# Two reorderings at once in a fused attention and mixture-of-experts kernel: the attention's first units with the later norms, and the expert stage's places

## The reference

```python
mod = (silu(c) @ wmod).reshape(4, 6, 1, 256)            # sa, ca, ga, sb, cb, gb
ga, gb = clamped gates: sign * max(|g|, 0.25)
h = layernorm(x) * (1 + ca) + sa
x = x + ga * attention(h)       # 16 heads of 128, causal, softmax, then W_O
h = layernorm(x) * (1 + cb) + sb
x = x + gb * ffn(h)
# ffn: down 256->128, router with 8 experts (top 2 of a softmax), a shared
# expert, 8 experts of hidden width 128..512 with gelu before and after w1,
# their sum weighted by the gates, up 128->256, plus gelu(h) @ core
```

## Time and profile before

| | |
|---|---|
| median of 3 runs | 800.54 us (799.82 to 801.06) |
| time of the profiled execution | 800.14 us |
| its span | 798.2 us |
| PE busy in the span | 776.1 us (97%) |
| weight loads (PEld) | 690.7 us (87%) |
| DVE busy | 662.0 us (83%) |
| ACT busy | 624.9 us (78%) |
| POOL busy | 462.6 us (58%) |
| PE on the chain that ended last | 79% |

### The profile page before, as it was taken

The page is one execution under the profiler, slowest core; times in us unless marked ns, Lnnn a source line. Parts: engine busy times, 40 slices in busy tenths (PEclk is TensorE's granted clock), DMA queues, the critical chain, the costliest instruction groups (busy, mean ns, idle before and its releaser), DMA issues.

```text
span 798.2 us, 14365 instructions
## 1 busy us (share of the span) xinstructions
PE 776.1 (97%) x4700; PEld 690.7 (87%) x4700; DVE 662.0 (83%) x1649; ACT 624.9 (78%) x1449; POOL 462.6 (58%) x389
## 2 busy tenths in 40 slices
PE   8899999999999999999999999999999899989997
PEld 7689989999999999999999999999999677768786
DVE  4779998878888878888878888879898988786967
ACT  3787889877777888777888877887879868866974
POOL 2454456765557666555576655575445365677654
PEclk8999999999999999999999999999999999999999
DMA  7252233442223444223343332344222131112231
GB/s 250 83 171 69 67 93 96 113 105 67 67 67 71 101 111 120 70 67 70 84 106 93 93 93 69 85 110 133 69 67 67 48 119 55 53 41 68 75 98 53
DMA packets 47593, 70.53 MB, mean 88 GB/s; under 512 B 5536, under 2 KB 38464, under 8 KB 47392
## 3 DMA queue, kind: packets, MB, share of 16 engines
q1 hardware_dynamic: 47008, 68.81, 32.9%
q0 software_dynamic: 368, 0.81, 0.3%
q10 hardware_dynamic: 144, 0.00, 0.0%
HBM read 25.49 MB, written 2.17 MB: 35 GB/s over the span
## 4 chain that ended last, share of the span: by engine, by line
PE 79%; ACT 8%; DVE 7%; issue 3%; POOL 2%; DMA 1%; SPq 0%; DVEq 0%; POOLq 0%
PE M L759 12%; PE M L760 12%; PE M L758 12%; PE T L758 8%; PE T L760 8%; PE T L759 8%; PE S L758 5%; PE S L760 5%; PE S L759 5%; PE M L864 2%; ACT PB L696 1%; ACT PB L647 1%; PE S L849 1%; POOL stage L565 1%; DMA PB<-in_wmod 1%
## 5 line engine op out<-in xcount | busy, mean ns | idle before, releaser
L604 POOL TENSOR_TENSOR ptl<-ptl,pth 128x896 fp32r<-128x896 f32 x126 | 179.7, 1448 | 94.7 <-ACT pth L726 94.7
L696 ACT ACTIVATE PB<-PB,ri 128x256 f32<-128x256 f32 (+3 forms) x256 | 123.2, 553 | 30.4 <-DVE ri L1180 30.3
L647 ACT ACTIVATE PB<-S,nb 128x128 f32<-128x128 f32 (+3 forms) x256 | 135.2, 540 | 7.1 <-DVE nb L1171 6.9
L1160 DVE TENSOR_TENSOR qk<-M,qk 128x512 fp32r<-128x512 f32 x108 | 74.2, 687 | 58.8 <-ACT qk L711 58.7
L592 POOL TENSOR_TENSOR X<-X,fb 128x512 f32<-128x512 f32 x64 | 83.2, 1300 | 61.1 <-DVE fb L1207 61.0
L1171 DVE CUSTOM_DVE_ANT_0 S<-S,cc 128x128 f32<-128x128 f32 (+3 forms) x256 | 117.3, 520 | 1.3 <-PE S L760 1.3
L711 ACT CAST qk<-M 128x512 fp32r<-128x512 f32 x108 | 64.3, 595 | 67.0 <-PE M L760 67.0
L1187 DVE STREAM_TRANSPOSE gab<-PB 128x256 f32<-128x256 f32 (+2 forms) x192 | 109.5, 624 | 6.7 <-DMA ptl<-gab 2.2
L760 PE MATMUL M<-hh,W 128*128 128x512 f32 x222 | 87.5, 394 | 0.0
L759 PE MATMUL M<-hl,W 128*128 128x512 f32 x222 | 87.3, 393 | 0.0
L758 PE MATMUL M<-hh,W 128*128 128x512 f32 x222 | 86.8, 391 | 0.5 <-DVE hl L1146 0.5
(11 more groups left out here) (264 smaller groups left out, 2491.8 us busy)
## 6 DMA issues: line engine op xcount, KB each, us to landing
ptl<-gab SPq DMA_DIRECT2D x256, 160.0 KB, 3.1
stage<-in_wat SPq DMA_DIRECT2D x16, 512.0 KB, 5.1
gab<-scw SPq DMA_DIRECT2D x16, 256.0 KB, 3.2
tmp<-scw SPq DMA_DIRECT2D x16, 256.0 KB, 3.4
X<-in_x SPq DMA_DIRECT2D x3, 512.0 KB, 8.2
stage<-in_wfa SPq DMA_DIRECT2D x3, 512.0 KB, 4.8
out<-X SPq DMA_DIRECT2D x3, 512.0 KB, 2.6
X<-in_wmod SPq DMA_DIRECT2D x1, 1024.0 KB, 12.1
```

What stands on the lines that cost most here:

```text
L604: pool.tensor_tensor(pt_part(lo, c), pt_part(lo, c).bitcast(F32), pt_part(hi, c).bitcast(F32), ALU.subtract).then_inc(s_pl, 1)
L647: ins = act.activation(PB[:, P_OFF[i]:P_OFF[i] + w], PS[bk][:, a:a + w], ACT.Exp, bias=nb[:, i:i + 1], scale=-1.0, accum_out=sm[:, i:i + 1])
L696: act.activation(p, p, ACT.Copy, scale=ri[:, i:i + 1]).then_inc(s_P3, 1)
L1160: v.tensor_tensor(lo, src, hi.bitcast(F32), ALU.subtract).then_inc(me, 1)
```

## The change

It changes only the order of events, and who makes one low half. In the attention:

- In the first units, `v` 0 is made ahead of `nm` 1, the gate's product `mg` moves from ahead of S 1 to behind `v` 0,1, `k` 2 comes ahead of `ri` 1, and `h` for batch 1 moves from the end of pass 0 into its middle (behind S 2 and behind ty 2).
- The exponentials of unit 1 follow the rule of the later units.
- The two halves of `nm` for norms 2, 3, 4 and 5 move from behind S and q to behind wo and v of the same pass.

In the expert stage, `st` 6 comes one place earlier, `nb` 6 and `nm` 6,0 too, `wo` 31 one or so later; the low half of W piece 21 goes from DVE to POOL; and `dn` 2 comes ahead of `rs` 2,10 instead of behind `rs` 2,12.

```diff
         if b == 1:
-            put(pre, i, ("h", b, 0))
-            put(post, i, ("h", b, 1))
+            put(mid, (i, 0), ("h", b, 0))
+            put(mid, (i, 1), ("h", b, 1))
...
-        fill[i + 1] = [[("nm", b, 0)], [("nm", b, 1)]]
+        fill[i + 1] = [[], [], [("nm", b, 0)], [("nm", b, 1)]]
...
-        fill[55 + 4 * b] = [[("nm", B + b, 0)], [("nm", B + b, 1)]]
+        fill[55 + 4 * b] = [[], [], [("nm", B + b, 0)], [("nm", B + b, 1)]]
...
-        ("q", 1), ("ri", 0), ("k", 1), ("norm", 0), ("nb", 1), ("ty", 0), ("nm", 1, 0), ("nm", 1, 1), ("v", 0, 0),
-        ("mg",), ("tr", 0), ("S", 1), ("q", 2), ("ri", 1), ("k", 2), ("norm", 1), ("ty", 1), ("pt", 0), ("mh",), ("v", 0, 1),
-        ("wh", 3), ("tr", 1)]
+        ("q", 1), ("ri", 0), ("k", 1), ("norm", 0), ("nb", 1), ("ty", 0), ("v", 0, 0), ("nm", 1, 0), ("nm", 1, 1),
+        ("tr", 0), ("S", 1), ("q", 2), ("k", 2), ("ri", 1), ("norm", 1), ("ty", 1), ("v", 0, 1), ("pt", 0), ("mg",),
+        ("wh", 3), ("mh",), ("tr", 1)]
...
-    put(0, 6, ("wt", 0), ("wl", 0), ("wl", 1), ("wl", 2), ("d0", 0))
-    put(0, 7, ("z", NU - 1), ("st", 6, 0), ("st", 6, 1), ("d0", 1))
-    put(0, 8, ("wo", last, 0), ("st", 6, 2), ("st", 6, 3), ("d0", 2))
-    put(0, 9, ("wo", last, 1), ("wl", 3), ("nb", 6))
-    put(0, 10, ("nm", 6, 0))
-    put(0, 11, ("dn", 1), ("nm", 6, 1))
+    put(0, 6, ("wt", 0), ("wl", 0), ("wl", 1), ("wl", 2), ("st", 6, 0), ("st", 6, 1), ("d0", 0))
+    put(0, 7, ("z", NU - 1), ("st", 6, 2), ("st", 6, 3), ("d0", 1))
+    put(0, 8, ("nb", 6), ("d0", 2))
+    put(0, 9, ("wo", last, 0), ("nm", 6, 0))
+    put(0, 10, ("wo", last, 1), ("wl", 3), ("nm", 6, 1))
+    put(0, 11, ("dn", 1))
...
+    put(1, 17, ("dn", 2))
...
-        if t + 1 < B:
+        if t == 2:
             put(t, 17, ("dn", t + 1))
...
-BY_V = (0, 1, 21, 22)
+BY_V = (0, 1, 22)
...
-                        exps(ev[1] - 1, [1, 2] if ev[1] == 2 else [0, 1])
-                    if kind == "k" and ev[1] >= 3:
+                        exps(ev[1] - 1, [0, 1])
+                    if kind == "k" and ev[1] >= 2:
                         exps(ev[1] - 1, [2])
```

More of the change, by code:

```diff
@@ L712, in _ @@
                     if kind == "q" and ev[1] >= 2:
-                        exps(ev[1] - 1, [1, 2] if ev[1] == 2 else [0, 1])
-                    if kind == "k" and ev[1] >= 3:
+                        exps(ev[1] - 1, [0, 1])
+                    if kind == "k" and ev[1] >= 2:
                         exps(ev[1] - 1, [2])
-                elif kind == "ex" or kind == "S" and ev[1] < 2:
-                    u = ev[1]
-                    exps(u, [0] if u == 1 else [0, 1, 2])
+                elif kind == "ex" or ev == ("S", 0):
+                    exps(ev[1], [0, 1, 2])
                 elif kind == "ra":
@@ L1274, in _ @@
                         if t == 0:
-                            v.wait_ge(s_wd, 1 + BY_V.index(21))
+                            lo_done(v, 21)
                             v.tensor_scalar(acc_at(t), PT[n % 2][:], 0.1, bc[:, B_SH2:B_SH2 + 1], ALU.mult,
```

## The result

The changed kernel takes 808.46 us (median of 4 runs, 807.08 to 811.57) against 800.18 us (4 runs, 797.93 to 801.06) of the kernel before on the same chip; the ratio is 1.0113 with an interval of 0.9 to 1.4% (1.0088 to 1.0137). The profiled execution took 807.08 us (span 805.2 us, 7.0 us more than before).

The account below looks back on a forecast made before the run. PE was taken as the bound, busy 776.1 of 798.2 us. Attention +5.4, expert start -1.1 and dn 2 -2.2 gave +2.1 on 800.14, or 802.3, stated as 802.4 us; range 797.2 to 805.2.

Parts of the forecast that it names:

- First units, -2.5: Start of attention: the new order lets S 4 start about 2.5 us earlier, bounds 1 to 3.5 us.
- Norm 2, 0 with the first units' gain used up: Attention, h of batch 2: PE's wait uses up the first units' gain; 0, bounds -1.5 to +1.0 us.
- norm 3, +1.0: Attention, h 3: S 9's 1.20 us wait goes, but POOL's piece 4 delays nm; +1.0 us (0 to +2).
- norms 4 and 5, +2.2 each: Attention, h2 of batches 0 and 1: nm halves meet POOL's operations, h2 2.2 us late each; +4.4 us.
- The low bound: Norms 4 and 5: the second half of nm behind the lo of v makes h2 0.6 us late per norm.
- the third rival: At the four h's, PE's clock falls in the new waits, at two of four costing 2.6 us: 805 us; chance 0.13.
- The expert start, -1.1: Start of expert stage: piece 21's gain goes again, h2 no longer waits 1.02 us; -1.1 us, bounds 0 and -3.3.
- dn 2, -2.2: Expert stage: the 3.05 us wait goes, wt 2 starts near 713.5 instead of 715.45, matmuls at full speed; -2.2 us.
- the first rival: The new places of nm cost PE nothing, h2 of batch 1 under 1 us late: 795 to 797 us; chance 0.23.
- the second: About even: better expert stage bound, or norm 2 keeps 1.5 us of the first units' gain: 800.2 us; chance 0.27.

Follow-up runs that it names:

- e8: Changed kernel with POOL's subtraction for pt's low half cut to 16 columns at units 4, 7, 56 and 60; the four h waits 7.0 us together.
- e9: e8 with POOL's addition to X also cut to 16 of 512 columns at four places; single run, h waits 0.55, 1.59, 0.55 and 0.55 us.
- e4: Changed kernel with the halves of nm 2 to 5 at their old places and the low half of piece 21 back on DVE; 795.52 us.
- e2: Kernel before with only the new places of the halves of nm 2 to 5; 811.35 us.
- e3: Changed kernel with only the low half of W piece 21 back on DVE; 808.26 us.
- e10: Kernel before with only the new places of st, nb and nm 6 and of wo 31; ratio 0.9987 (0.9973 to 1.0002).
- e11: Kernel before with only the low half of piece 21 moved to POOL; 801.54 us, ratio 1.0013 (0.9992 to 1.0034).
- e6: Kernel before with only dn 2 moved from the end of its tile to its start; 797.39 us.
- e7: e4 with both halves of nm 2 to 5 placed behind wo, ahead of ty; 795.47 us.

## Why the prediction was right in the mechanism and wrong in the size

From S 0 to the last row of PE the profile shows +8.8 us (780.68 against 771.90) where my sum was +2.1. By kind, 3.6 us of the 8.8 are idle time of PE (-1.1, +7.4 and -2.6 in the three stretches) and 5.1 us are busy time for the same matmuls, so the clock (0, +3.3 and +1.9). My sum held 3.4 us of waits and took off 1.3 us of clock (in the term for `dn` 2). The waits came out as forecast, in part by luck, since their errors of up to 1.4 us cancel; the step that failed is the clock, which the sum put at nothing behind four forecast waits of more than 2 us and behind piece 21. By its own steps:

1. **First units, -2.5.** Measured -1.1 against the profile that I added to. S 2 came 2.0 us earlier as said (14.40 us behind S 0 instead of 16.41), but by S 4 half of it was gone: z 1 waited 1.24 us for POOL's `pt` (the row at 53.41), which stands behind the gate's four operations and on which I had put 0.8 us, and z 0 waited 0.64 us, which I had not foreseen. Against the other executions of the old order the gain is 2.7 us, 1.6 of them for a reason that the prediction did not have: it ends the fall of the clock behind the wait before S 2. I had written that this wait does not bring the clock down; the one execution that I had did not show it, four others do.
2. **Norm 2, 0 with the first units' gain used up; norm 3, +1.0; norms 4 and 5, +2.2 each.** Waits of 2.09, 2.31 less the 1.2 us of S 9 that are saved, 2.08 and 2.09 us: the mechanism, the place and the size are right. e8 and e9 show both meetings with POOL by themselves. The low bound that I gave for the order alone, 0.6 us, was 0.55 us.
3. **The clock in these waits, not in the sum.** This is the largest error. S 4 to S 63 costs 10.6 us, the waits 7.4 of them (8.57 less 1.20); the remaining 3.3 us are PE's busy time (553.16 against 549.89), in the two stretches at 1.2 GHz, some 1.65 us each. e8, with waits of 1.49 to 2.50 us and a granted clock of 1.00 in the windows behind all four, has nothing left over: 556.91 - 550.46 = 6.45 us, the waits 7.02 - 0.71 (e4's wait before S 9) = 6.31. Of the twelve waits of 2.08 to 2.76 us before an h in after, e2 and e3, seven were followed by a stretch at 1.2 GHz. I had this as the third rival, "the clock falls in the new waits", at two of four and 2.6 us, with a chance of 0.13: it should have been part of the forecast, since I myself forecast waits above 2 us.
4. **The expert start, -1.1.** Measured +1.4: norm 6 gives 0.71 us (e10), piece 21 costs 2.07 us (e11). The second step that failed is "the next step of this kind (L1056) would wait for POOL's new 2.4 us. So DVE loses about 2.2 us". Two instructions in a row were held, L1055 by piece 21 and L1056 by the first subtraction of `pt` 63, 4.3 us in all. The timelines of DVE and PE in the kernel after are those of e11:

```profile
638.27 2.29 DVE L1055 CAST wgw<-wg 128x64 fp32r<-128x64 f32 x1
640.60 2.00 DVE L1056 TENSOR_TENSOR wgw<-wg,wgw 128x32 fp32r<-128x32 f32 x1
...
643.25 0.79 PE L758 MATMUL S<-ur,W 128*128 128x512 f32 x1 [2.67 <-DVE G4l L1332]
```

   The 3.0 us that DVE gains by not doing the piece come behind G4l: the loss stands ahead of PE's next need, the gain behind it. Over the whole stretch the two did cancel in PE's idle time, as I had netted them (8.89 us in e11 against 8.90). But the loss came as one wait of 2.65 us, and the 2.07 us are the clock behind it. In the same way norm 6 saved 1.94 us of waits, more than the 1.02 that I had named, and lost 1.23 us to a fall of the clock without a wait. So in idle time this term is -1.95 us, and the clock, 3.3 us, makes +1.4 of it.
5. **dn 2, -2.2.** Measured -2.03 alone (e6): the wait went to `wt` 2 and shrank as worked out, 0.78 us; the other 1.25 us are the clock, which I had right by luck, since it fell at this wait in four of nine executions. In the changed kernel `wt` 2 waits 1.67 us, the clock did not fall there, and the three edits of the expert stage sum as measured alone: 2.07 - 0.71 - 2.03 = -0.67 against -0.78.

The errors add up: 3.3 (clock) + 1.4 (first units) + 2.5 (expert start) + 0.2 (dn 2), less 0.5 for h waits a little shorter than forecast (7.4 us net against 2.5 + 5.4), is 6.9 us; 8.8 - 2.1 is 6.7. Of these, 3.3 + 2.07 + 1.23 = 6.6 us are the clock, and the errors of the waits nearly cancel. That the first rival (h without a wait) and the second (about even) failed is shown by the rows at L808.

The Trainium skill ("SBUF — State Buffer", Who interferes with whom) names `cast`, and `tensor_tensor` with both inputs in SBUF, beside `tensor_scalar` as instructions that contend with GpSimd for an exclusive lock; L1055 at 2.30 against 0.20 us and L1056 at 1.99 against 0.19 us agree. I had applied the rule to `nm` and to L1056 and had left out the cast between.

## What to carry to other kernels

When an instruction moves to another engine that locks against this one, list every instruction of this engine that falls into the new operation and into what comes behind it there, and see whether the loss and the gain stand ahead of the same wait: if not, the waiting may be the same in total, but gathered in one long wait. Price a forecast wait of 2 us or more on TensorE with the clock behind it, here 1.3 to 1.65 us in somewhat more than half of the cases and up to 2.1 us behind the wait of 2.65 us. Read the idle and the busy time of TensorE apart, stretch by stretch, before a difference is put down to waiting, and look at more than one execution before saying that a wait leaves the clock alone. If work of DVE is moved later in its row, put all of it in one place ahead of the last thing that PE needs before it: with the second half behind `v` S 4 to S 63 took 10.6 us more than before, with both behind `wo` nothing more.

## What the runs showed of the hardware that was not expected

Waits of the same size are followed by a stretch at 1.2 GHz or not: 2.31 us at 111.13 in the kernel after left the clock at 1.00 (110 to 120 us), 2.08 us at 566.62 did not. Over the 14 profiled executions, from S 0 on, the clock fell at (during, or within 1.6 us behind) all nine waits of PE of 2.65 us and more, at 15 of the 26 of 1.77 to 2.52 us, and at none of 1.67 us and less. What decides among those in the middle is open. And the clock also fell where PE had not been idle: at 694 us of the kernel after, about 1 us behind the sixteen matmuls of 16 columns of the router and with no wait between, as this window shows (granted clock 0.83, PE busy 9.90 of 10 us):

```profile
690.00:700.00 10.00, 9.90 (x45) 7.96 (x44) 7.80 (x17) 7.57 (x14) 2.25 (x3) 0.83 0.01 2
```

The same happened behind the same sixteen matmuls in e10 and e7; in the eleven other executions it did not (e3 and e4 show 1.00 from 690 to 700 us). The three have the new places of norm 6, but so have five of the eleven; the cause is open. Such falls, of 1.3 to 1.65 us each, and the start, which alone moved S 0 by 2.8 us, make the time of one execution uncertain, so that effects of 1 us could be told only by stretches between two instructions of PE, and there by its idle time, not by the runs.
